# One program block for a graph-attention stage and the three attention layers behind it

## What is computed

```python
def gat(x, adj):                                  # round 0, 12 heads of 32
    h = einsum('bnd,ade->bane', x, W); th = tanh(h)
    attn = th @ w_src + swap(th @ w_dst)          # one source and one target score a node
    attn = where(attn >= 0, attn, 0.2 * attn); attn = where(~adj, -999., attn)
    out = elu(softmax(attn) @ h + b)
    gate = sigmoid(x @ H_w.T + H_b)
    return gate * out + (1 - gate) * x
def att(x, adj):                                  # rounds 1 to 3, 6 heads of 64
    q, k, v = heads(x @ Wq + bq), heads(x @ Wk + bk), heads(x @ Wv + bv)
    probs = softmax(q @ k.T / 8 + where(adj, 0, -9e15))
    return merge(probs @ v) @ Wf + bf
x = layernorm(x + gat(x, adj))
for _ in range(3): x = layernorm(x + att(x, adj))
```

## Time and profile before

| | us |
|---|---|
| median of 3 runs | 3042.13 (3039.78 to 3043.57) |
| the profiled execution | 3042.37, its span 3040.6 |

### The profile page before, as it was taken

How to read it: one execution, slowest core, us unless ns; L and a number is a source line. 1 busy time by engine, 2 the same in 40 slices (tenths; PEclk the granted TensorE clock), 3 DMA queues, 4 the chain that set the end, 5 groups by cost and what they waited for, 6 DMA issues and landing times. The chain is left out here.

```text
span 3040.6 us, 72404 instructions
## 1 busy us (share of the span) xinstructions
PE 2947.9 (97%) x22432; PEld 2633.9 (87%) x22432; DVE 2569.7 (85%) x8653; ACT 2416.6 (79%) x6892; POOL 1257.5 (41%) x1239
## 2 busy tenths in 40 slices
PE   7999999999959999999999999999999999999997
PEld 6888888888759999999999999999999999999996
DVE  5999999999848888888888888888888888888886
ACT  6999999999947777777777777777777777777775
POOL 2666666666623332323224343332323323232232
PEclk9999999999979999999999999999999999999998
DMA  2111111111032222222232222222222222222221
GB/s 80 35 35 35 35 35 35 35 35 35 23 96 73 71 73 79 74 78 76 75 105 72 78 76 77 71 72 78 76 78 73 72 78 73 78 76 75 73 72 48
DMA packets 153212, 198.84 MB, mean 65 GB/s; under 512 B 48896, under 2 KB 115456, under 8 KB 152320
## 3 DMA queue, kind: packets, MB, share of 16 engines
q1 hardware_dynamic: 152832, 194.20, 23.1%
HBM read 68.31 MB, written 50.33 MB: 39 GB/s over the span
## 5 line engine op out<-in xcount | busy, mean ns | idle before, releaser
L969 POOL TENSOR_TENSOR a_residual<-a_x,a_br 128x384 f32<-128x384 f32 x192 | 190.2, 1011 | 1383.5 <-DVE a_mix L1159 1369.3
L1041 ACT ACTIVATE a_probs<-a_logits,a_nmax 128x256 f32<-128x256 f32 x1152 | 574.0, 503 | 5.8 <-DVE a_nmax L1131 0.9
L1131 DVE CUSTOM_DVE_ANT_0 a_logits<-a_s,a_mask 128x256 f32<-128x256 f32 x1152 | 432.9, 420 | 99.6 <-PE a_s L1289 96.6
L89 PE MATMUL a_pj<-a_xt_hi,a_w_lo 128*128 128x256 f32 x1728 | 493.5, 286 | 4.3 <-DVE a_xt_lo L1112 4.3
L90 PE MATMUL a_pj<-a_xt_lo,a_w_hi 128*128 128x256 f32 x1728 | 485.2, 281 | 0.0
L91 PE MATMUL a_pj<-a_xt_hi,a_w_hi 128*128 128x256 f32 x1728 | 485.1, 281 | 0.0
L350 ACT ACTIVATE g_exps<-g_v,g_nmax 128x256 f32<-128x256 f32 x768 | 384.7, 513 | 3.0 <-DVE g_nmax L520 0.5
L1152 DVE TENSOR_SCALAR a_probs<-a_probs,a_recs 128x256 f32<-128x256 f32 x1152 | 365.2, 359 | 20.5
L1026 ACT ACTIVATE a_split<-a_pj,a_bc 128x256 fp32r<-128x256 f32 x576 | 241.5, 470 | 160.7 <-PE a_pj L91 160.6
L1034 ACT ACTIVATE a_stack<-a_split 64x512 fp32r<-64x512 f32 x576 | 360.3, 625 | 3.4
L1048 ACT ACTIVATE a_pt_copy<-a_pt 128x512 f32<-128x512 f32 x288 | 172.0, 597 | 232.3 <-PE a_pt L1299 229.9
(11 more groups left out here) (120 smaller groups left out, 8089.0 us busy)
## 6 DMA issues: line engine op xcount, KB each, us to landing
a_stack<-a_split SPq DMA_DIRECT2D x576, 128.0 KB, 2.4
a_x<-y SPq DMA_DIRECT2D x96, 384.0 KB, 3.1
y<-a_out SPq DMA_DIRECT2D x96, 384.0 KB, 2.7
g_x<-x SPq DMA_DIRECT2D x32, 384.0 KB, 3.1
y<-g_out SPq DMA_DIRECT2D x32, 384.0 KB, 2.5
w_stage<-att_w SPq DMA_DIRECT2D x3, 2304.0 KB, 10.5
a_adj<-adj SPq DMA_DIRECT2D x96, 64.0 KB, 3.0
g_adj<-adj SPq DMA_DIRECT2D x32, 64.0 KB, 3.0
```

Source lines behind the costliest of these rows:

```text
L89: pe.matmul(out, a[1], b[0], start=first, stop=False)
L1041: last = act.activation(probs[:, (HEADS * u + h) % 4, t, :], logits[:, h % 2, t, :], ACT.Exp, scale=-1.0, bias=nmax[:, u, h, t:t + 1], acc ...
L1131: last = dve.tensor_tensor_reduce(out=logits[:, h % 2, t, :], in0=s_ps[h % 2][:, t, :], in1=mask[u][:, t, :], scale=-HEAD_DIM ** -0.5, sca ...
```

## The change

`gat_phase` and `attention_phase` become one function `network` with one block. Names of the first stage get the prefix g_ in the code. Its last two slots and the layers' two opening slots are taken out of the lists and written anew as `crossing_0` and `crossing_1` on each engine: in `crossing_0` the first stage's last sample (`g_odd`) is current, its last but one (`g_even`) is finished and sample 0 of the layers (`first`) is projected; in `crossing_1` `g_odd` is finished, `first` is current and sample 1 (`second`) projected. Full slots keep their order of work.

- Tiles: x, adjacency, identity, xT, residual, mix, statistics and out are shared by both stages; the layers' other tiles lie on space that the first stage uses earlier or not at all. PSUM banks are the same tiles for both.
- The first layer's weights are split by GpSimd (`split_weights(0, part)`), one twelfth after each of the first twelve full slots of the first stage, not by ScalarE and VectorE. `w_stage` becomes two tiles, `w_whole0` and `w_whole1`. In the layers the parts move from full slots 0 to 11 to slots 6 to 17, and the loads of the next weights behind the fourth sample of a layer.
- SP: the loads of `first` and `second` stand in the first stage's queue, as soon as `g_x_used` says that the tile is free; the stores of `g_even` and `g_odd` stand behind the moves of `first` and of `second`.
- Bias loads come at the program's start; `k_lo` is zeroed in `crossing_0`.

```diff
-    slot(None, (0, 0), None, (0, 0, 0), opening=True)
-    slot((0, 0), (0, 1), None, (0, 0, 0), opening=True)
...
+            held(sp, g_x_used, at(1, *g_even, 1), passed)
+            sp.wait_ge(g_stored[0], 16 + START)
+            load(*first)
+            g_store(HALVES - 2, 1)
+            held(sp, g_x_used, at(1, *g_odd, 1), passed)
+            sp.wait_ge(g_stored[1], 16 + START)
+            load(*second)
...
                 for pair in range(2):
                     for u in range(2):
                         behind = pair - 2 + u
+                        sample(begin + pair, u, behind % HALVES if layer or behind >= 0 else None, pair + 1)
+                        if layer == 0 and pair == 0:
+                            g_store(HALVES - 1, u)
...
+            for pair in range(HALVES - 1):
+                g_slot((pair, 1), (pair + 1, 0), (pair, 0))
+                if 2 * pair < PARTS:
+                    split_weights(0, 2 * pair)
+                g_slot((pair + 1, 0), (pair + 1, 1), (pair, 1))
+                if 2 * pair + 1 < PARTS:
+                    split_weights(0, 2 * pair + 1)
...
             def add_back(half, u, t):
+                if (half, u, t) == (0, 0, 0):
+                    dve.wait_ge(g_ln_done, at(NT, *g_odd, NT))
```

The crossings: of `crossing_0` ScalarE's order, the end of VectorE's and TensorE's, of `crossing_1` VectorE's and TensorE's, in this sequence:

```diff
+            def crossing_0():
...
+                g_relu(*g_odd, 2)
+                g_relu(*g_odd, 3)
+                high_xt(*first, 0)
+                high_xt(*first, 1)
+                g_exp(*g_odd, 2)
+                g_copy_ct(*g_even, 2)
+                g_relu(*g_odd, 4)
+                g_relu(*g_odd, 5)
+                g_exp(*g_odd, 3)
+                g_relu(*g_odd, 6)
+                g_exp(*g_odd, 4)
+                g_even_pt(*g_odd, 1)
+                high_qk(*first, 0, 0)
+                g_exp(*g_odd, 5)
+                g_relu(*g_odd, 7)
+                copy_v(*first, 0)
+                g_exp(*g_odd, 6)
+                g_exp(*g_odd, 7)
+                g_copy_ct(*g_odd, 0)
+                g_relu(*g_odd, 8)
+                g_relu(*g_odd, 9)
+                high_qk(*first, 1, 0)
+                g_even_pt(*g_odd, 2)
+                g_exp(*g_odd, 8)
+                g_elu_exp(*g_even)
+                g_relu(*g_odd, 10)
+                g_relu(*g_odd, 11)
+                copy_v(*first, 1)
+                g_even_pt(*g_odd, 3)
+                g_exp(*g_odd, 9)
+                g_exp(*g_odd, 10)
+                own_rows(*first, 0)
+                high_qk(*first, 2, 0)
+                g_exp(*g_odd, 11)
+                g_even_pt(*g_odd, 4)
+                g_copy_ct(*g_odd, 1)
...
+            def crossing_0():
...
+                g_maximum(*g_odd, 10)
+                g_maximum(*g_odd, 11)
+                g_elu_and_gate(*g_even)
+                g_odd_pt(*g_odd, 3)
+                low_qk(*first, 2, 0)
+                g_statistics(*g_even)
+                g_odd_pt(*g_odd, 4)
+
+            def crossing_1():
+                g_odd_pt(*g_odd, 5)
+                low_xt(*second, 0)
+                low_xt(*second, 1)
+                mask_and_max(*first, 0)
+                mask_and_max(*first, 1)
+                g_invert(*g_odd)
+                mask_and_max(*first, 2)
+                normalise(*first, 0)
+                mask_and_max(*first, 3)
+                low_qk(*second, 0, 0)
+                normalise(*first, 1)
+                g_divide(*g_odd, 0)
+                low_qk(*second, 1, 0)
+                g_divide(*g_odd, 1)
+                mask_and_max(*first, 4)
+                normalise(*first, 2)
+                normalise(*first, 3)
+                g_elu_argument(*g_odd)
+                odd_pt(*first, 0)
+                mask_and_max(*first, 5)
+                normalise(*first, 4)
+                g_elu_and_gate(*g_odd)
+                low_qk(*second, 2, 0)
+                odd_pt(*first, 1)
+                g_statistics(*g_odd)
...
+            def crossing_0():
...
+                g_scores_of(*g_odd, 4)
+                g_scores_of(*g_odd, 5)
+                pe.wait_ge(g_gate_done, at(NT, *g_odd, NT))
+                make_qk(*first, 0, 0, True)
+                g_scores_of(*g_odd, 6)
+                g_pair_of_transposes(*g_odd, 1)
+                make_v(*first, 0, 0)
+                g_scores_of(*g_odd, 7)
+                pe.wait_ge(pj_read, split_of(*first, QK[0]))
+                g_make_back(*g_even, 0, g_odd, None)
+                g_four_contexts(*g_odd, 0)
+                g_pair_of_transposes(*g_odd, 2)
+                pe.wait_ge(v_read, at(NT, *first, 1))
+                g_make_back(*g_even, 1, g_odd, None)
+                g_scores_of(*g_odd, 8)
+                g_scores_of(*g_odd, 9)
+                make_qk(*first, 1, 0, True)
+                g_scores_of(*g_odd, 10)
+                pe.wait_ge(g_back_read, at(NT, *g_even, 1))
+                make_v(*first, 1, 0)
+                g_scores_of(*g_odd, 11)
+                g_pair_of_transposes(*g_odd, 3)
+                pe.wait_ge(g_back_read, at(NT, *g_even, NT))
+                make_qk(*first, 2, 0, True)
+                g_four_contexts(*g_odd, 1)
+                g_pair_of_transposes(*g_odd, 4)
+
+            def crossing_1():
+                g_pair_of_transposes(*g_odd, 5)
+                transpose_x(*second, 0, True)
+                transpose_x(*second, 1, True)
+                pair_of_scores(*first, 0)
+                g_four_contexts(*g_odd, 2)
+                make_qk(*second, 0, 0, True)
+                pair_of_scores(*first, 1)
+                make_v(*second, 0, 0)
+                pe.wait_ge(pj_read, split_of(*second, QK[0]))
+                g_make_back(*g_odd, 0, None, None)
+                make_qk(*second, 1, 0, True)
+                pe.wait_ge(v_read, at(NT, *second, 1))
+                g_make_back(*g_odd, 1, None, None)
+                pair_of_scores(*first, 2)
+                pair_of_transposes(*first, 0)
+                pe.wait_ge(g_back_read, at(NT, *g_odd, 1))
+                make_v(*second, 1, 0)
+                pe.wait_ge(g_back_read, at(NT, *g_odd, NT))
+                make_qk(*second, 2, 0, True)
+                pair_of_transposes(*first, 1)
```

1364 lines of the change are left out of this document (703 added, 661 removed).

## The result

| | us |
|---|---|
| the changed kernel, median of 4 runs | 3009.97 (3009.13 to 3011.11) |
| the kernel before beside it, median | 3041.14 (3039.78 to 3043.57) |
| ratio, 95% interval | 0.9894 (0.9882 to 0.9906) |
| profiled execution, its span | 3011.11, 3009.3 |

Forecast was 3011. The windows by stage of the changed kernel, with the same columns as the earlier trace rows. The borders are ScalarE's first relu of `g_odd`, a point 1.1 us ahead of the `x` transposes of the layers' second sample (850.5), and the first `x` transposes of the first full slot; then that slot, one steady slot of the layers and one of the first stage. The border at 849.40 is a choice between two engines' orders, so only the sum of the first two is a clean measure.

A forecast was written before the change was run, and what follows sets the result against it. Steady slots were bound by ScalarE (first stage) and TensorE (layers) and stay unchanged; the join's 88.6 us becomes 57.5, saving 31.1 from 3042.4, so 3011 us. Forecast case 3006 to 3015, range 3000 to 3019.

The forecast's parts named there:

- the stretch: From ScalarE's start on `g_odd` (813.57) to the layers' first full slot (902.15): 88.6 us, to be replaced by two crossings.
- The walk: Written orders of both crossings followed with handoffs between engines: 33.4 us for crossing_0, 59.3 us for both.
- my choice: Both crossings taken at 57.5 us, between 55.1 without handoffs and 59.3 with them, as handoffs and durations partly overlap.
- Its waits: ScalarE in crossing_0: `relu 6` 1.4 us, `copy_ct 0` and `relu 8` 1.2, `high_qk 1` 1.7; VectorE in crossing_1: 2, 2.3, 2.
- GpSimd's splits at nothing: First stage, slots 2 to 13: idle time before `g_mix` covers 1.52 us a slot; cost 0, or 18 us without cover.
- Port contention at nothing: GpSimd's splits slow VectorE by 0.44 us each, under its 2.43 us idle per first-stage slot; cost 0.
- all 18 us: By the skill's rule on the shared Vector port, all 18 us of GpSimd's splits could fall on VectorE.
- SP's order at nothing: Stores of the last two samples between the moves of `first` and `second`: 0, or 2 us if `g_even`'s norm is late.
- B: Rival: the crossings' orders hide the waits, only busy time counts, 47.6 us, saved 41.0, 3001 us; chance 0.19.
- C: Rival: TensorE's clock falls in the crossings, half the work at half clock, about 8 us longer, 3019 us; chance 0.11.
- D: Rival: new waits serialise the crossings, only the seam goes, 61.2 us, saved 27.4, 3015 us; chance 0.10.
- E: Rival: new tile addresses slow TensorE-bound slots; 0.33 us per slot loses the gain, 0.5 gives 3058 us; chance 0.02.

The follow-up runs named there:

- order runs: The changed kernel with steps reordered in crossing_0, then crossing_1 too, then TensorE's order too: 3007.89, 3007.48 and 3002.71 us.
- split_before_spread: The changed kernel with GpSimd's twelve weight splits moved within their slots, ahead of the spread targets instead of behind the norm: 3011.25 us.
- order_pe: The changed kernel with steps reordered in both crossings on ScalarE and VectorE, and TensorE's own order matched to them: 3002.71 us, ratio 0.9867.

## Why the prediction came out right

**What bounds the kernel, and the stretch: right.** All of the gain lies between 813.57 and the second full slot, but for 2.5 us of slots and 3.4 us of the end. The steady slots kept their bounds.

**The walk was near, in part by luck, and the choice below it too low.** The walk gave 59.3 us, measured are 60.1 (with VectorE's `odd_pt 4`, the walk's end of crossing 0, done at 33.6 for 33.4). I took 57.5, on the ground that the handoffs partly overlap with durations. That is the term that was mis-sized, by 2.6 us. But the walk was made at the full clock, and 1.45 us of the 60.1 are the half clock: without them the same order took 58.7, 0.6 less than the walk and 1.2 more than my choice. So some overlap was real; I took off too much for it, and nothing was on the other side for the clock.

**Its waits, one by one.** On ScalarE the walk said 1.4 for `relu 6`, 1.2 for `relu 8` and 1.7 for `high_qk 1`; measured are 1.1, 0.9 and 1.5. The walk missed that TensorE waits for the split of `qk 0` before `g_make_back(even, 0)` (1.47 us), and saw the end of VectorE's queue only as the last transposes' wait, not the contexts' (3.04). In crossing 1 `elu_exp` waited 3.04 us. The first full slot's transposes waited 3.8, where I had the 1.83 of before. So its sum came near with single waits missed. The order runs show what these waits were worth: the stretch fell to 58.2, 55.3 and 50.8 us, and with the first full slot, which took over some of the work, from 84.5 to 82.2, 80.3 and 75.4.

**3010 instead of 3011 is luck, two errors that cancel:** the stretch 2.6 us too short in the forecast, and 2.9 us that I had not in the sum (slots -2.5, end -3.4, start +2.5, first full slot +0.5; the start differs in the same way between two profiles of one kernel, the end by 2.6 us). Without the slots' 2.5 us the median would have been near 3012.5, still in the forecast's own range.

**GpSimd's splits at nothing: right for another reason.** The cover is the wait for `g_cx`, not that for `g_mix`. And late spreads cost 1.3 us, not 18: in `split_before_spread` they come later by 1.5 us in twelve slots, and the slots grow by 0.1 us each. I priced a delay on GpSimd as if it went through to the end of the slot, without a row that showed a consumer waiting.

**Port contention at nothing: right for the steady slots** (22.25 us with parts and without), where each engine off the bound has slack. In `order_pe`, at the crossing, it lengthened VectorE's work by 2.1 us, and TensorE waited 1.4 us behind it. The Trainium skill (Advanced Engine Details and Errata, VectorE Performance Modes) has GpSimd's instructions and VectorE's two-port ones (2p) block each other on the shared port. The 2.73 us against 0.62 agree; so does `xt_lo`, which reads PSUM and kept its 0.54 us beside the same GpSimd work. The prediction's "all 18 us" left that limit out.

**SP's order at nothing: right**; no wait for a DMA is on TensorE's list.

**The rivals.** *B* (3001) did not happen with the order as written, but `order_pe` came to 3002.7. What I held against it, that waits in the chain of score, relu and maximum are not filled by work elsewhere in the queue, held for this order only: much of them went when steps whose inputs come late were moved back. *C*: the clock did fall, but for 3.4 us from 850.0 and 6.8 us from 873.9 only, where C had half of the work at half of the clock. It cost 1.45 us in the stretch and 2.1 in the slot behind it, where the kernel before paid 1.6; C had 6 to 8. *D* was right in that most of the gain needs no weave (22.8 of 31 us). Its sum was 12.7 us short, 8.4 of it in one term: 14.6 us for the opening slot, which left out that VectorE still has the first stage's end ahead of it. It is 23.0 there, and 18.2 with the copies moved ahead. *E*: no steady slot grew. The sign was the other one, -0.027 us, a twelfth of the 0.33 at which E would decide.

**What was to be seen:** no idle time of TensorE over 7 us (3.8 at most); crossings of 33 and 25 us (33.4, 26.8); parts on GpSimd from 92.8 to 369.9 us at 0.507 + 1.022 us (row below); the first full slot at 871 (876.2, as the start was 2.5 us late and the crossing 2.6 long):

```profile
L520 POOL TENSOR_TENSOR w_lo<-w_whole,w_hi x12: 1014/1022/1033, 92.8 to 369.9; 128x384 fp32r<-128x384 f32 x12
```

## What to carry to other kernels

Where two stages are joined, first remove the seam (here 23 of 31 us), and then read each engine's queue at the join for a step that waits while ready work stands behind it: three such passes over a finished weave, none of which removed any work, were worth 7 us more by the raw medians, 9 by the sums and 10 by the distance to the kernel before, some of it by the clock. Sum a hand walk with its handoffs from start to start, and don't take it down by feel. Before a delayed helper is given a price, find in the trace who waits for it; and price a half clock only where others wait for the engine: there it is paid nearly in full, elsewhere it can cost nothing.

## What the runs showed of the hardware

- A pair of VectorE's scalings of 128x256 took 2.73 us beside GpSimd's additions of 128x768 and 128x384, and 0.62 alone. It looks as if VectorE was held until GpSimd's instruction had ended (867.96 + 1.82 = 869.78); `xt_lo`, with an input in PSUM, kept its length beside the same work (0.54).
- The same slot took 22.280 or 22.300 us with no change but where tiles lie, 1.8 us over 92 slots. In the program with one block it took 22.253; whether that is placement too is open.
- 3.4 us of half clock (1.2 GHz) cost 1.45 us of a woven stretch over work that others waited for, 3.5 us nothing at another place of the same order. A slot in which TensorE had no gap grew from 22.3 to 24.4 us at a mean clock of 0.91.
- The clock at start and end is not the program's: two profiles of the changed kernel, with the same instructions, had 3.4 us of half clock at 27 us and none there, and their ends took 61.5 and 64.1 us.
